# Attention's first 512 rows completed on the chip instead of through memory

## The reference, cut to what matters

```
x = x + L0_xattn(layernorm(x), ctx)     # linear, with a bias from ctx
x = x + L0_ffn(layernorm(x))            # 8 experts, each takes its top 512 rows
x = x + L1_xattn(layernorm(x), ctx)     # attention, 16 heads of 16, 154 keys
x = x + L1_ffn(layernorm(x))            # quantized gate/up/down, width 768

# L0_ffn: a row may be taken by several experts, or by none
top_vals, token_idx = top_k((x_flat @ Wg.T).T, 512)
h = silu(xg @ W1.T) * (xg @ W3.T)
y = (h @ W2.T) * softmax(top_vals)
out = zeros.at[token_idx].add(y)
```

## Time and profile before

| | us |
|---|---|
| median of 3 runs (758.94 to 761.31) | 760.51 |
| the profiled execution | 759.17 |
| its span on the core | 757.3 |
| TensorE busy | 640.5 (85%) |
| VectorE busy | 622.8 (82%) |
| ScalarE busy | 530.3 (70%) |
| GpSimd busy | 308.1 (41%) |

### The profile page before, as it was taken

The page is one execution under the profiler, slowest core; times in us unless marked ns, Lnnn a source line. Parts: engine busy times, 40 slices in busy tenths (PEclk is TensorE's granted clock), DMA queues, the critical chain, the costliest instruction groups (busy, mean ns, idle before and its releaser), DMA issues.

```text
span 757.3 us, 12157 instructions
## 1 busy us (share of the span) xinstructions
PE 640.5 (85%) x4243; PEld 385.4 (51%) x4243; DVE 622.8 (82%) x1304; ACT 530.3 (70%) x713; POOL 308.1 (41%) x249
## 2 busy tenths in 40 slices
PE   6983038999999789999999999999998996029998
PEld 5762024666555544466455645644443444006887
DVE  5898897998999699886887877989897999995433
ACT  2134564777675648888998996666657996996873
POOL 4336603477777627360343120014412443892000
PEclk9997559999999999999999999999999999559999
DMA  9945664466753580000041001021102413101443
GB/s 300 321 152 200 208 169 142 120 146 166 190 134 56 89 289 1 1 23 1 1 149 34 1 29 40 18 83 56 56 0 112 167 55 112 56 0 56 147 133 112
DMA packets 59542, 78.17 MB, mean 103 GB/s; under 512 B 7904, under 2 KB 48224, under 8 KB 59488
## 3 DMA queue, kind: packets, MB, share of 16 engines
q1 hardware_dynamic: 49936, 60.58, 24.4%
q0 software_dynamic: 7872, 14.82, 9.0%
q10 hardware_dynamic: 1680, 2.08, 0.8%
HBM read 50.07 MB, written 27.39 MB: 102 GB/s over the span
## 4 chain that ended last, share of the span: by engine, by line
PE 58%; DVE 16%; ACT 10%; POOL 3%; issue 2%; DMA 1%; POOLq 0%; DVEq 0%
PE bank L2569 10%; PE bank L2303 8%; PE bank L2247 8%; PE bank L2601 5%; PE bank L1584 4%; PE bank L1641 4%; PE bank L1626 3%; PE bank L1694 3%; DVE above L850 2%; PE bank L1656 2%; DVE qx L1307 2%; ACT wgateT L2196 2%; PE bank L1599 2%; PE bank L1665 2%; PE bank L1621 2%
## 5 line engine op out<-in xcount | busy, mean ns | idle before, releaser
L1307 DVE TENSOR_REDUCE qx<-bank 128x4 f16<-128x616 f32 x128 | 98.0, 801 | 22.1 <-PE bank L1584 20.4
L1440 ACT ACTIVATE x<-bank,bic 128x512 f32<-128x512 f32 x160 | 104.6, 690 | 15.9 <-PE bank L1626 12.1
L2247 PE MATMUL bank<-ux,uwh 128*128 128x512 f16 x384 | 92.7, 384 | 0.0
L2247 PEld LDWEIGHTS bank<-ux,uwh 128*128 128x128 f16 x384 | 38.0, 99 | 46.8 <-issue 2.8
L1584 PE MATMUL bank<-Kb,qTb 128*128 128x308 bf16 x256 | 52.5, 297 | 2.0 <-DVE qx L1307 1.1
L2247 PE MATMUL bank<-ux,uwl 128*128 128x512 f16 x192 | 49.9, 383 | 0.0
L1232 POOL CAST qx<-q 128x1024 f16<-128x1024 f32 x8 | 8.5, 1066 | 98.3 <-PE bank L1599 87.3
L1626 PE MATMUL bank<-qT,K 128*128 128x512 f16 x128 | 44.4, 380 | 0.3
L2303 PE MATMUL bank<-uwh,oh 128*128 128x256 f16 x192 | 44.1, 276 | 0.0
L2303 PE MATMUL bank<-uwl,oh 128*128 128x256 f16 x192 | 44.1, 275 | 0.0
L2254 PE MATMUL bank<-uwh 128*128 128x512 f16 x39 | 12.9, 501 | 36.1 <-DVE peak L1977 36.1
(11 more groups left out here) (459 smaller groups left out, 1876.0 us busy)
## 6 DMA issues: line engine op xcount, KB each, us to landing
x_dram<-x SPq DMA_DIRECT2D x4, 1024.0 KB, 5.3
xr<-in_w1T SPq DMA_DIRECT2D x8, 512.0 KB, 3.8
xr<-in_w3T SPq DMA_DIRECT2D x8, 512.0 KB, 4.9
xr<-in_w2T SPq DMA_DIRECT2D x8, 512.0 KB, 6.4
row_dram<-xn SPq DMA_DIRECT2D x8, 512.0 KB, 3.0
x_dram<-xr SPq DMA_DIRECT2D x8, 512.0 KB, 3.0
x<-x_dram SPq DMA_DIRECT2D x8, 512.0 KB, 4.7
xT<-in_xT SPq DMA_DIRECT2D x7, 512.0 KB, 7.8
```

The lines of the kernel that those rows point to most:

```text
L1307: dve.tensor_reduce(qx[:, k, g * GH:(g + 1) * GH, MROW].rearrange("p (u h) -> p u h", u=2), pair[i][:].rearrange("p (u x) -> p u x", u=2)[ ...
L1440: act.activation(dst, S_[u % 2], ACT.Exp, bias=bic[:, s // 2, int(tail):int(tail) + 1], scale=1.0 / 16).then_inc(p_done, 1)
L2247: mm = pe.matmul(bank[j][:, m * TB:(m + 1) * TB], w[:, c * HI + cols:c * HI + cols + P], x[:, part, c * TB:(c + 1) * TB], start=(w is uwh ...
```

## The change

The last expert's results reach the first 512 rows twice: on the chip for attention, and in memory, as before, for completeness of the other rows.

- SyncE loads the numbers 0 to 511 (`tokens`, the same in each partition, 256 KB) while expert 6's last products run. GpSimd compares them with the last expert's row numbers: `token_mark[p, k, t]` is 1 where slot p of group k holds row t (`marked_rows`, four operations of 128x512, placed before expert 6's scatter).
- The first 512 rows are loaded in one DMA as soon as the scatters of experts 0 to 6 have landed. The last expert's scatter waits until they are on the chip (`rows_in[0]`), and the other seven slices' loads wait, as before, until that scatter has landed.
- ScalarE makes the high half of `yw` (`yh`), VectorE the low one (`yl`); TensorE multiplies the marks by both into `direct` (32 products, type F32R); VectorE adds `direct` to `xr` in two halves (`completed_rows`) and goes on with the statistics.
- Gathers wait for the gates' copy (`e_ys`, made in `row_gates` at the expert's start) instead of the results.
- The key masks of batch 1 go one by one into VectorE's order in experts 6 and 7, the key heads into ScalarE's; the key remainders go to GpSimd, after slice 2's queries (`key_remainders_gpsimd`).
- TensorE's first dummies go from 22 to 4. The transposes of the last block's weights use other banks, and the last evictions stand behind the first copy of turned queries. VectorE's first string changes from `smmmms...` to `mmsmms...`.

```diff
@@ constants
+    tokens = np.broadcast_to(np.arange(4 * P, dtype=np.float32), (P, 4 * P)).copy()
@@ keys
+        def key_remainders_gpsimd(pool, raw, K, Kr, b):
+            pool.wait_ge(k_hi, NKH * (b + 1))
+            pool.wait_ge(q_q, 3 * QT)
+            pool.tensor_scalar(raw[0][:], raw[0][:], any16[:, b:b + 1], None, ALU.mult).then_inc(k_own, 1)
+            pool.wait_ge(k_own, CT + 2)
+            for h in range(2):
...
+                pool.tensor_tensor(K[rows, :, h, :], raw[0][rows, :, 0:P], K[rows, :, h, :], ALU.subtract).then_inc(k_lo, 1)
+                for a in range(2):
+                    pool.wait_ge(k_lo, made + 1 + a)
+                    pool.tensor_tensor(key_tail(Kr, rows, h, a), raw_tail(raw[0], rows, a), key_tail(Kr, rows, h, a), ALU.subtract).then_inc(k_lo, 1)
@@ attention_sync
+                sp.wait_ge(e_put, PUT - 16 * CT)
+                sp.dma_start(xr[:, 0:QT, :], tiles(x2_dram)[:, 0:QT, :]).then_inc(rows_in[0], 16)
                 sp.wait_ge(e_yw, YW)
+                sp.wait_ge(d_direct, 2)
                 value_loads(sp, 0)
...
                 sp.wait_ge(e_put, PUT)
-                for t in range(0, QT, 2):
-                    sp.dma_start(xr[:, t, :], tiles(x2_dram)[:, t, :]).then_inc(rows_in[t], 16)
-                for t in range(QT):
-                    sp.wait_ge(rows_in[t], EARLIER + 16)
@@ attention_vector
+                def completed_rows():
+                    dve.wait_ge(rows_in[0], EARLIER + 16)
+                    for n in range(QT // 2):
+                        dve.wait_ge(d_direct, n + 1)
+                        x = xr[:, 2 * n:2 * n + 2, :]
+                        dve.tensor_tensor(x, x, direct[:, 2 * n:2 * n + 2, :], ALU.add).then_inc(d_added, 1)
...
-                keys(1, "mask")
-                keys(1, "remainders")
...
+                completed_rows()
                 statistics(0)
@@ attention_scalar
-                for h in range(2):
-                    key_heads(act, raw, K[1], Kr[1], 1, h)
...
                 cast(0)
+                act.wait_ge(e_put, PUT - 16 * CT)
+                for g, (cols, place) in enumerate(DOWN_PLACES):
+                    act.wait_ge(f_wt, 2 * DC + g + 1)
+                    act.activation(wdownT[:, cols, :], place.rearrange("p (c d) -> p c d", d=D), ACT.Copy,
+                                   scale=qs[:, WS + 2:WS + 3]).then_inc(f_cp, 1)
@@ attention_tensor
+                pe.wait_ge(k_own, 1 + CT)
+                for k in range(CT):
+                    for part, made in ((yh, d_high), (yl, d_low)):
+                        pe.wait_ge(made, k + 1)
+                        for t in range(QT):
+                            mm = pe.matmul(direct[:, t, :], token_mark[:, k, t * P:(t + 1) * P], part[:, k, :],
+                                           start=(part is yh and k == 0 and t % 2 == 0), stop=(part is yl and k == CT - 1), skip_group_check=True)
+                            if part is yl and k == CT - 1 and t % 2:
+                                mm.then_inc(d_direct, 1)
                 pe.wait_ge(e_yw, YW)
                 for i in range(2):
                     for c in range(DC):
+                        if i == c == 1:
+                            pe.wait_ge(d_added, QT // 2)
...
-                pe.wait_ge(e_put, PUT)
-                kept_running(22)
+                kept_running(4)
@@ sync, gpsimd
+                    sp.wait_ge(e_h, (E - 1) * HC)
+                    sp.dma_start(tokens[:], a["tokens"]).then_inc(rows_in[1], 16)
...
                             pool.wait_ge(e_xT, e + 1)
-                            pool.wait_ge(e_yw, e * CT + CT)
+                            pool.wait_ge(e_ys, e - 1)
...
+                    def marked_rows(pool):
+                        pool.wait_ge(e_wl, 10 * E + 20)
+                        pool.tensor_copy(last_rows, idx[:, E - 1, :]).then_inc(k_own, 1)
+                        pool.wait_ge(rows_in[1], EARLIER + 16)
+                        pool.wait_ge(k_own, 1)
+                        for k in range(CT):
+                            pool.tensor_scalar(token_mark[:, k, :], tokens[:], last_rows[:, k:k + 1], None, ALU.is_equal).then_inc(k_own, 1)
...
+                        if e == E - 2:
+                            marked_rows(pool)
                         if e == E - 1:
                             pool.wait_ge(e_y, e + 2)
-                            attention_clears(pool)
+                            pool.memset(qb[:, :, :, HD + 1:MW], 0.0).then_inc(k_set, 1)
+                            pool.wait_ge(rows_in[0], EARLIER + 16)
                         if e:
                             pool.wait_ge(e_put, e * (16 * CT))
                             pool.sem_inc(e_free, 1)
                         scattered(e)
+                    pool.wait_ge(d_direct, QT // 2)
+                    attention_clears(pool)
@@ vector, last expert's results
                             for k in range(CT):
+                                if k == 2:
+                                    key_mask(2)
+                                    row_lo(0)
+                                    row_lo(1)
+                                if k == 3:
+                                    key_mask(3)
+                                    row_lo(2)
                                 dve.wait_ge(e_y, e + 3 + k)
-                                dve.tensor_scalar(yw[i][:, k, :], last_y[k], xg[i][:, k, D + e:D + e + 1], y_scale, ALU.mult, ALU.mult).then_inc(e_yw, 1)
+                                dve.tensor_scalar(yw[i][:, k, :], last_y[k], row_gates[:, k:k + 1], None, ALU.mult).then_inc(e_yw, 1)
+                            row_lo(3)
@@ scalar, last expert
+                            if not more and c < 3:
+                                key_head(act, raw, K[1], 1, c // 2, c % 2)
                             h_hi(e, c)
```

More of the change, by code:

```diff
@@ L275, in build @@
         identb, identr = sb(resid, "identb", [P, P], BF16), halves(resid, "identr", [P, P])
-        k_in, k_set, k_kb, k_hi, k_lo, w_in = (sem("key_" + n) for n in "in set kb hi lo w".split())
+        k_in, k_set, k_kb, k_hi, k_lo, k_own = (sem("key_" + n) for n in "in set kb hi lo own".split())
         g_mask, g_mk = sem("g_mask"), sem("g_mk")
@@ L1085, in build @@
             wmaxes = peak[:, 0:E * QE]
+            last_rows, direct = qs[:, 4:4 + CT], bank[2][:].rearrange("p (k d) -> p k d", d=D)
+            d_direct, d_added, d_high, d_low = (sem("last_" + n) for n in "direct added high low".split())
             WS, WI, XW, OUT = 16, 19, 22, 24
@@ L1119, in build @@
             sb(st, "rows_place", [P, 32])
+            with ExitStack() as last:
+                token_mark = sb(last, "token_mark", [P, CT, 4 * P], F32R)
+                tokens = sb(last, "tokens", [P, 4 * P])
             qx = halves(st, "qx", [P, QT, HEADS, SW])
@@ L1122, in build @@
             rden = sb(st, "rden", [P, QT, GH])
+            with ExitStack() as last:
+                sb(last, "weights_place0", [P, 64])
+                yh, yl = (sb(last, f"y{part}", [P, CT, D], F32R) for part in "hl")
             qT = [halves(st, f"qT{i}", [P, PR, QT, P]) for i in range(2)]
@@ L1530, in work @@
                         act.wait_ge(q_var, 1)
[L1531 removed]
+                        act.activation(root[:, t], var[:, t], ACT.Sqrt).then_inc(q_act, 1)
                     if c == "W":
@@ L2463, in expert @@
                                 h_lo(e, c)
+                            if c == 2 and not more:
+                                key_mask(1)
                             if more and c:
@@ L2468, in expert @@
                             rows_lo(e + 1, 1 - i)
+                        if more == 1:
+                            key_mask(0)
                         if not more:
```

110 lines of the change are left out of this document (70 added, 40 removed).

## The result

The changed kernel takes 762.46 us (median of 20 runs, 758.84 to 764.37); the kernel before, run beside it, 760.45 (20 runs, 757.82 to 762.34). The ratio is 1.0024, with a 95% interval of 1.0016 to 1.0033: 1.2 to 2.5 us slower. The profiled execution has 762.46 and a span of 760.7, against 759.17 and 757.3.

The account below looks back on a forecast made before the run. Bound: VectorE's second statistics behind the queries, ending at 277.42 us. Expert 6's scatter at 243.8 plus 32.7 gives 276.5, a gain of 0.9; profiled 758.3, plus 1.34 to the median, 759.6 us; whole range 756.0 to 763.4.

Parts of the forecast that it names:

- The sign: Whole kernel: a gain of 0.9 us to 759.6; chances 0.33 faster, 0.50 the same, 0.17 slower.
- Part 1: Expert 5's scatter, no longer held, starts about five microseconds sooner; expert 6's scatter then has a floor of 240.24 us.
- Part 2: Four marks on GpSimd before expert 6's scatter: 2.0 us each, 8.0 in all, so that scatter starts at 243.8.
- Part 3: First 512 rows completed on chip after expert 7: 32 products at 140 ns, first query cast at 265.1, 4.2 us sooner.
- Part 4: Other rows arrive after two scatter-and-load trips: second statistics end 32.7 us after expert 6's scatter starts, at 276.5, gaining 0.9.
- rival (a): The forecast case at GpSimd's marks: slow form, gain 0.9 us, 759.6; chance 0.45.
- Part 5: Batch 1's key remainders, 7.2 to 10.4 us, fit GpSimd's 11.05 us idle time after slice 2's queries; otherwise the split is late.
- The clock, costed at nothing: TensorE from 255 to 264 us: clock expected to hold, cost nothing; half clock for the first maxima would cost 2 or 3.
- (b): GpSimd's marks take only 0.6 to 1.1 us each, expert 6's scatter stays at its floor: gain 3.1, 757.4; chance 0.30.
- (c): Marks short but TensorE's new products at 219 ns, query cast 2.2 us later: gain 0.9, 759.6; chance 0.08.
- (d): Second trip of rows longer, four scatters taking 9.6 us: loss 2.9, 763.4; chance within a shared 0.17.
- (e): Gathers' new order changes nothing, marks start at 239.4: loss 2.7 us, 763.2; chance within a shared 0.17.

Follow-up runs that it names:

- e5: Changed kernel with six unused 512-column products filling TensorE's wait for VectorE near 279 us; 761.97 us, ratio 1.0025.
- e1: Changed kernel without GpSimd's key remainders of batch 1 (left out altogether, semaphores still raised); 759.25 us, ratio 0.9987.
- e8: Changed kernel with GpSimd's key remainders taken apart: scaling behind the first split, subtraction halves behind the queries of slices 1 and 2; 760.73 us, ratio 1.0002.
- e13: Kernel before, with two additions of 16 partitions by 1024 columns and one scaling on GpSimd behind slice 2's queries; 764.31 us, ratio 1.0047.
- e2: Changed kernel with the four marks behind expert 6's scatter on GpSimd instead of ahead of it; 761.02 us, ratio 1.0001.
- e6: Changed kernel with the second slice of the later rows signalling on its own semaphore; 759.32 us, ratio 0.9986.
- e7: Changed kernel with e6's own semaphore, e8's key remainders taken apart, and three dummies at TensorE's wait near 279 us; 758.04 us, ratio 0.9973.
- e9: Changed kernel with e6's own semaphore and e8's key remainders taken apart, without dummies; 756.29 us, ratio 0.9952.
- e10: e7 plus nine unused 512-column products in TensorE's wait at the first expert's start, against the changed kernel; 756.15 us, ratio 0.9936.
- e14: The changed kernel itself, unaltered, run and profiled again; 761.55 us, ratio 1.0023.
- e12: Kernel before, with six query instructions of 1.2 us repeated on GpSimd behind slice 2's queries; 760.29 us, ratio 0.9994.
- e11: Kernel before, with the second slice of the later rows on its own semaphore; 760.53 us, ratio 0.9994.

## Why the prediction was wrong, by its own steps

**The sign.** The forecast was a gain of 0.9 us and "the same". Measured is a loss of 1.2 to 2.5 us. What the traces show is this: the start of attention gains 0.3 to 1.0, the hold costs 1.7, and the fall of the clock near 279 us costs some 1.2 in the executions that have it. That makes a loss of 0.7 to 1.4 us without the fall and of 1.9 to 2.6 with it. It is a sum from single profiles; in what share of the executions the clock falls is not known, and e5 speaks against a large one.

**Part 1**, right. Expert 5's scatter no longer holds anything; expert 6's is set by the marks.

**Part 2**, right in kind, mis-sized. A mark takes 1.55 us where 2.0 was taken and 0.61 to 2.26 given as bounds: 2.7 ns a column by the prediction's fixed 0.18 us, neither fast nor slow. They also began later, at 2.07 us before expert 6's results and not 2.5: they wait for VectorE's last reading of the scales and then for a cast, which no step of mine had. Expert 6's scatter came at 4.30 behind its results (5.46 forecast). The estimate from the Trainium skill, "GPSIMD Engine Reference", section "Performance pitfalls for Q7 kernels", about 1 us a mark, fell short too.

**Part 3**, right. The new products come every 113 ns (32 in 3.6 us). The weight load's 140 was no floor: the loads of these products show 188 ns each in the trace, beside the products before them, and the products keep their pace. The first query cast comes 5.4 us sooner in its own terms, 4.2 forecast. One thing was missed: GpSimd's MEMSET of 1.48 us, at 266.00, stands beside the casts. The first of them starts at 266.35 and ends at 267.63, 0.15 us behind the MEMSET, and the other three take 0.40 each. In e2, by chance, the MEMSET is over (266.32) before the casts start (266.99), and the four take 1.38 again; in e6, e7, e9 and e10 they take 2.18 to 2.52, the more the longer the MEMSET still runs. So the same kind of hold costs 0.8 to 1.1 us here.

**Part 4**, right in its mechanism, and the heart of it, but the size that came out is in part luck. The second statistics end 33.75 us behind expert 6's scatter (32.7 forecast): the two loads took 8.3 us and not 6.9 until slice 3 had landed, and 0.8 us pass between the first rows' landing and the next scatter; the second four scatters, 7.1 us, were shorter. With the marks 1.2 us early and the trip 1.05 late, the two errors cancel, and the forecast gain of 0.9 came out as 1.03 in this pair of profiles, as rival (a) has it. I put the third slice into the sum as something that the statistics need, and did not see that they only wait for it because of a shared semaphore; that was worth 1.6 us.

**Part 5** is the step that failed: "It fits; if not, the split comes late by the excess." It does fit: 9.5 us of work where 7.2 to 10.4 were taken, and the split is not late by it. But the only cost that the step knew was on GpSimd. The runs showed it on VectorE, 1.68 us between the norms and the added rows (e1, e8, e13), which the prediction put at nothing. Fitting an idle gap says nothing of the engine beside it. A sign was at hand in VectorE's timeline of the kernel before: four key masks took 3.26 us, and 4.71 where GpSimd was busy with a split. The two timelines:

```profile
328.57 4.71 DVE L293 TENSOR_TENSOR Kb<-kbraw,kbm 32x616 bf16<-32x616 f32 x4
```

```profile
329.80 1.28 POOL L1232 CAST qx<-q 128x1024 f16<-128x1024 f32 x1 [5.92 <-PE bank L1599]
331.02 1.60 POOL L1233 CAST qx<-q 128x1024 f16<-128x1024 f32 x1
332.60 2.67 POOL L1235 TENSOR_TENSOR qx<-q,qx 128x1024 f16<-128x1024 f32 x1
```

The first two masks took 0.8 us each, the last two 1.52 each (from 330.20 and from 331.76), and ended 0.65 us behind the end of a cast (331.72 and 331.07, 333.28 and 332.62). The casts, 1.04 us each when alone, took 1.28 and 1.60 here. By these times the two engines took turns, and each lost.

**The clock, costed at nothing**, failed as well, in the executions in which it falls (e14). I looked at TensorE's share from 255 to 264 us, where it held (1.00, TensorE busy 9.00 of 9 us). The fall is 15 us later, in the wait which Part 4 foretold on VectorE (2 us) and whose effect on TensorE I did not follow.

**The rivals.** (b) and (c) fell with the marks and products as measured. The slower side was given 0.17, for a longer second trip (d), old gathers (e) and the clock together; of these only the clock happened, and the largest cause was not among them. That the measured 762.46 lies inside the whole range, 756.0 to 763.4, is luck: the range reached that far for (d), which did not happen.

## What to carry to other kernels

Work that is moved into an engine's idle time must be held against the rows of the neighbour beside it: on GpSimd, look up what VectorE does in the same microseconds, and put long GpSimd instructions where VectorE reads from PSUM or waits. When a change makes an early part earlier, ask which wait then comes last, and whether it waits for more than it needs; a semaphore that two loads share is cheap until the loads are late. A wait that the change puts on one engine is to be followed to TensorE.

## What the runs showed of the hardware

- A VectorE operation of 0.16 us on SBUF data took up to 1.89 us beside a GpSimd instruction of 1.9 to 2.8 us and ended with it, within 0.04 us in eight cases of five kernels (1.71, 0.36 changed; 1.71, 0.36 e6; 0.43 e8; 0.34 e7; 1.86, 0.65 e13). Subtract-and-multiply instructions of 1.2 us on GpSimd held nothing (0.26 at most, e12). Beside the scaling of 128x1232 the sum took 0.72, ending 0.36 us before it.
- An equality mark of 128x512 floats on GpSimd took 1.55 us, and 1.9 beside busy VectorE.
- Products of 256 columns with fp32r operands came every 113 ns, beside weight loads of 188 ns each.
- TensorE's granted clock fell from 2.4 to 1.2 GHz in or just behind a wait of 2.0 to 2.4 us in four profiles and did not in one with 2.15. It did not in the twelve profiles whose longest wait there was 1.6 us or less.
- Four casts of 128x256 on VectorE took 1.38 us, and 2.25 where a GpSimd MEMSET of 1.48 us was running at their start.
- Executions of one kernel differ in the clock: from 120 to 125 us it was 0.64 to 1.00 of full speed in four profiles of kernels that are the same up to there (before, e11, e12, e13), and expert 6's results came at 238.34 to 239.91 us.
